# An RWKV block and a gated feed-forward on one core: the constants of the time mixes made on ScalarE, GpSimd started by the norm, and three orders in the attention changed

## The reference, cut to what matters

```python
h  = layer_norm(x, ln1_g, ln1_b)
hh = time_shift(h)                                # the token before
k = (h * tm_mk + hh * (1 - tm_mk)) @ Wk.T         # the three time mixes r, k, v
v = (h * tm_mv + hh * (1 - tm_mv)) @ Wv.T
r = (h * tm_mr + hh * (1 - tm_mr)) @ Wr.T
x = x + sigmoid(r) * wkv(k, v, tm_first) @ Wo.T
h  = layer_norm(x, ln2_g, ln2_b)                  # and two more mixes, cr and ck
kk = (h * cm_mk + hh * (1 - cm_mk)) @ Wkey.T
x = x + sigmoid((h * cm_mr + hh * (1 - cm_mr)) @ Wcr.T) * (silu(kk) @ Wval.T)
x = x + ffn(layernorm(x))                         # silu(gate) * up, then down
```

## Time and profile before

| | us |
|---|---|
| runs | 1052.64, 1053.78, 1054.36 (median 1053.78) |
| profiled execution: own time | 1052.39 |
| its span in the trace | 1050.5 |
| PE busy in the span | 1041.9 |
| DVE, ACT, POOL busy | 704.9, 528.1, 616.7 |

### The profile page before, as it was taken

One profiled execution on the slowest core, in us unless ns is written; L12 is line 12 of the kernel. 1 busy time (PEld: TensorE's weight loads), 2 busy tenths in 40 slices (PEclk: granted clock), 3 DMA queues, 4 the chain that ended last, 5 costly groups with the idle time before them and its releaser, 6 DMA issues.

```text
span 1050.5 us, 13550 instructions
## 1 busy us (share of the span) xinstructions
PE 1041.9 (99%) x4680; PEld 861.8 (82%) x4680; DVE 704.9 (67%) x1215; ACT 528.1 (50%) x889; POOL 616.7 (59%) x508
## 2 busy tenths in 40 slices
PE   8999999999999999999999999999999999999999
PEld 7787888788888888888888888888888888888887
DVE  7899966786545564565459666767698566666655
ACT  7867887866444454323345434343435334444442
POOL 7796574635755545444447755578664356565552
PEclk9999999999999999999999999999999999999999
DMA  9100325177653344742323766575446445444432
GB/s 352 52 21 0 62 80 121 81 230 279 224 190 120 131 160 139 229 150 94 113 88 110 238 218 212 179 234 200 166 156 220 150 151 182 155 156 160 155 107 80
DMA packets 47333, 161.42 MB, mean 154 GB/s; under 512 B 5281, under 2 KB 5665, under 8 KB 42401
## 3 DMA queue, kind: packets, MB, share of 16 engines
q1 hardware_dynamic: 31808, 112.23, 30.8%
q0 software_dynamic: 15168, 48.24, 15.2%
q10 hardware_dynamic: 288, 0.09, 0.0%
HBM read 101.80 MB, written 58.74 MB: 153 GB/s over the span
## 4 chain that ended last, share of the span: by engine, by line
PE 91%; POOL 4%; DVE 3%; ACT 1%; issue 1%; DMA 0%; SPq 0%; DVEq 0%; ACTq 0%
PE bank L634 14%; PE bank L636 14%; PE bank L635 14%; PE bank L623 13%; PE bank L625 13%; PE bank L624 13%; PE bank L812 2%; PE bank L811 2%; PE bank L810 2%; POOL operand L2013 2%; POOL weights L2001 1%; PE bank L801 1%; POOL weights L2013 0%; DVE held L1548 0%; PE bank L698 0%
## 5 line engine op out<-in xcount | busy, mean ns | idle before, releaser
L634 PE MATMUL bank<-combo,left 128*128 128x512 f32 x672 | 262.4, 390 | 0.4 <-DVE bank L1732 0.4
L636 PE MATMUL bank<-combo,left 128*128 128x512 f32 x672 | 261.7, 389 | 0.0
L635 PE MATMUL bank<-combo,left 128*128 128x512 f32 x672 | 261.7, 389 | 0.0
L1663 DVE TENSOR_TENSOR resid<-bank,resid 128x512 f32<-128x512 f32 x176 | 120.6, 689 | 130.2 <-PE bank L625 129.4
L2086 POOL TENSOR_TENSOR inner<-made,inner 128x512 fp32r<-128x512 f32 x96 | 127.7, 1352 | 117.2 <-ACT inner L1135 117.1
L2046 POOL TENSOR_TENSOR left<-quart,left 128x512 fp32r<-128x512 f32 x96 | 115.3, 1225 | 83.6 <-ACT left L1098 43.2
L623 PE MATMUL bank<-right,inner 128*128 128x512 f32 x384 | 149.5, 389 | 0.0
L625 PE MATMUL bank<-right,inner 128*128 128x512 f32 x384 | 149.5, 389 | 0.0
L624 PE MATMUL bank<-right,inner 128*128 128x512 f32 x384 | 149.5, 389 | 0.0
L634 PEld LDWEIGHTS bank<-combo,left 128*128 128x128 f32 x672 | 126.2, 188 | 27.2 <-DVE bank L1732 1.1
L636 PEld LDWEIGHTS bank<-combo,left 128*128 128x128 f32 x672 | 126.2, 188 | 26.2
(11 more groups left out here) (202 smaller groups left out, 1972.8 us busy)
## 6 DMA issues: line engine op xcount, KB each, us to landing
kept_left<-left SPq DMA_DIRECT2D x24, 1792.0 KB, 8.2
left<-kept_left POOLq DMA_DIRECT2D x24, 1024.0 KB, 7.1
left<-kept_left POOLq DMA_DIRECT2D x24, 768.0 KB, 4.9
quart<-wide SPq DMA_DIRECT2D x24, 512.0 KB, 4.2
tall_staged<-tall SPq DMA_DIRECT2D x48, 256.0 KB, 4.9
raw<-kept SPq DMA_DIRECT2D x32, 256.0 KB, 6.2
landed<-wts SPq DMA_DIRECT2D x20, 256.0 KB, 5.5
resid<-x POOLq DMA_DIRECT2D x4, 1024.0 KB, 9.4
```

What stands on the lines that cost most here:

```text
L634: pe.matmul(acc[:], hi, combo[:, c, k, 0, :], start=fresh and k == 0, stop=False, skip_group_check=True)
L635: pe.matmul(acc[:], hi, combo[:, c, k, 1, :], start=False, stop=False, skip_group_check=True)
L636: mm = pe.matmul(acc[:], lo, combo[:, c, k, 0, :], start=False, stop=k == 1, skip_group_check=True)
L1663: dve.tensor_tensor(tile, A[s][:], tile, ALU.add).then_inc(added, 1)
```

## The change

It has five parts.

1. The constants of the mixes r, k and v are made by ScalarE in the new `first_shares`, twelve instructions of 128x3, when the vectors have landed and ahead of `matrix_hi(ITEM_R)`. VectorE makes those of cr and ck and the negated `tm_first` (`vec[:, 4]`) in the new `other_constants`, four instructions, now behind `norm1_moments(1)` and ahead of `mix("v", 0)`; its last line waits until they are done.
2. GpSimd waits for the first norm alone (`z1_ready`) ahead of its low parts of matrix r, and no longer for the constants.
3. In the blocks 2 and 3 ScalarE takes the gates 0 and 1 ahead of `mixed("k", b)`, and 2 and 3 behind it. Block 1 had this order already.
4. Between the third and the fourth `norm1_scaled` of the blocks 2 and 3 VectorE mixes the first tile of r.
5. In the mixes cr and ck of the blocks 0 to 2 VectorE takes the last tokens of the tiles 2 and 3 between the tiles of `mix_ck`, and no longer all ahead of it.

```diff
+FIRST_SHARES = 3 * KT
...
@@ rest_of, on ScalarE
                 act.wait_ge(transposed, KT * b + k + 1)
+                act.wait_ge(const_done, FIRST_SHARES + (4 if kind == "cr" else 0))
...
+            def first_shares():
+                share = vec[:, 5:8, :]
+                for k in range(KT):
+                    act.activation(whole_g[:, 0:3, k], share[:, :, k], ACT.Identity,
+                                   scale=vec[:, 0, k:k + 1]).then_inc(const_done, 1)
+                for k in range(KT):
+                    act.activation(whole_b[:, 0:3, k], share[:, :, k], ACT.Identity,
+                                   scale=vec[:, 1, k:k + 1]).then_inc(const_done, 1)
+                for k in range(KT):
+                    act.wait_ge(const_done, k + 1)
+                    act.activation(rest_g[:, 0:3, k], whole_g[:, 0:3, k], ACT.Identity, bias=vec[:, 0, k:k + 1],
+                                   scale=-1.0).then_inc(const_done, 1)
...
@@ wkv_weight, on ScalarE
                     act.wait_ge(k_psum, n + 1)
+                    act.wait_ge(const_done, FIRST_SHARES + 1)
...
@@ the order on ScalarE
             act.wait_ge(vec_loaded, 16)
+            first_shares()
             matrix_hi(ITEM_R)
-            act.wait_ge(const_done, 3)
+            act.wait_ge(const_done, FIRST_SHARES)
             mixed("r", 0, behind=1, amid=lambda: matrix_hi(ITEM_K, range(1)))
-            act.wait_ge(const_done, 7)
...
                 mix_hi("y", b - 1)
-                if b == 1:
-                    receptance_gate(b, range(2))
-                    mixed("k", b)
-                    receptance_gate(b, range(2, KT))
-                else:
+                if b > 1:
                     act.activation(table[:], minus_half[:, 0, 0:1], ACT.Sigmoid)
-                    mixed("k", b)
-                    receptance_gate(b)
+                receptance_gate(b, range(2))
+                mixed("k", b)
+                receptance_gate(b, range(2, KT))
...
@@ first_norm1, on VectorE
                 for s in range(SUBS):
                     normed(s)
-                shares(slice(0, 3), 0)
+
+            def other_constants():
+                dve.wait_ge(vec_loaded, 16)
                 dve.tensor_scalar(vec[:, 4, :], vec[:, 4, :], NO_STATE, -1.0, ALU.add, ALU.mult).then_inc(const_done, 1)
                 shares(slice(3, 5), 2)
+                dve.wait_ge(const_done, FIRST_SHARES + 4)
...
@@ the order on VectorE
             first_norm1()
             last_of_r_lo()
-            dve.wait_ge(const_done, 7)
+            dve.wait_ge(const_done, FIRST_SHARES)
             mix("r", 0)
...
             norm1_moments(1)
+            other_constants()
             mix("v", 0)
...
-                    norm1_scaled(b + 1, range(2, KT))
-                    mix("r", b + 1)
+                    norm1_scaled(b + 1, range(2, 3))
+                    mix("r", b + 1, range(1))
+                    norm1_scaled(b + 1, range(3, KT))
+                    mix("r", b + 1, range(1, KT))
...
             mix("cr", 0)
-            last_token(1, 0)
-            mix_ck(0)
+            last_token(1, 0, range(2))
+            for k in range(KT):
+                mix_ck(0, range(k, k + 1))
+                last_token(1, 0, range(k + 2, min(k + 3, KT)))
...
@@ the order on GpSimd
             first_norm1()
-            pool.wait_ge(const_done, 7)
+            pool.wait_ge(z1_ready, SUBS)
             matrix_lo(ITEM_R, range(KT - 1))
```

More of the change, by code:

```diff
@@ L1487, in norm1_scaled, with last_token @@
                     dve.tensor_tensor(bank_of, tile, scale, ALU.mult).then_inc(t1_psum, 1)
-            def last_token(norm, b):
+            def last_token(norm, b, tiles=range(KT)):
                 transposed, ms, beta = ((t1_psum, (0, 1, 2), 1), (t2_psum, (3, 4), 3))[norm]
-                for k in range(KT):
+                for k in tiles:
                     dve.wait_ge(transposed, KT * b + k + 1)
@@ L1501, in first_column, with mix @@
                 return (edge[:, b - 1, m, k:k + 1] if b else whole_b[:, m, k:k + 1])
-            def mix(kind, b):
+            def mix(kind, b, tiles=range(KT)):
                 n, m = operand_at(kind, b), MIXES[kind]
@@ L1514, in mix, with mix_ck @@
                                              in1=first_column(b, m, k), op0=ALU.mult, op1=ALU.add).then_inc(op_made, 1)
-            def mix_ck(b):
+            def mix_ck(b, tiles=range(KT)):
                 m = MIXES["ck"]
@@ L1949, in _ @@
             mix("cr", 0)
-            last_token(1, 0)
-            mix_ck(0)
+            last_token(1, 0, range(2))
+            for k in range(KT):
+                mix_ck(0, range(k, k + 1))
+                last_token(1, 0, range(k + 2, min(k + 3, KT)))
             gated_value(BLOCKS - 1)
             mix("cr", 1)
-            last_token(1, 1)
-            mix_ck(1)
+            last_token(1, 1, range(2))
+            for k in range(KT):
+                mix_ck(1, range(k, k + 1))
+                last_token(1, 1, range(k + 2, min(k + 3, KT)))
             mix("cr", 2)
-            last_token(1, 2)
-            mix_ck(2)
+            last_token(1, 2, range(2))
+            for k in range(KT):
+                mix_ck(2, range(k, k + 1))
+                last_token(1, 2, range(k + 2, min(k + 3, KT)))
             for s in range(SUBS):
```

2 lines of the change are left out of this document (1 added, 1 removed).

## The result

The kernel after takes 1055.79 us (median, 1054.60 to 1056.62); runs of before beside it had a median of 1053.77. The ratio is 1.0020, 95% interval 1.0013 to 1.0027: 2.1 us slower (1.4 to 2.8). 1056.7 had been predicted. The profiled execution of after took 1056.51, at the upper end of its runs, that of before 1052.39, near the lower end of its own; the pair differs by 4.12, twice what the medians show. Part of what follows separates the two.

The account below looks back on a forecast made before the run. PE, busy 1041.9 of 1050.5 us, was taken to bound the kernel. The terms 3.2 - 0.46 - 0.50 + 1.1 = +3.3, on the mean of 1053.3, gave 1056.6, stated as 1056.7, range 1053.0 to 1058.6.

Parts of the forecast that it names:

- GpSimd's earlier start: Low parts of matrix r: GpSimd gains 0.6, 0.35 arrives at PE's stop at 26.90, swallowed by the later delay.
- ScalarE's constants: Twelve small activations before the first weight copy take at most 2.4, until 7.2, while ScalarE sat idle: cost 0.
- Constants in front of the mix v: VectorE's four constants delay the mix v by 3.6 beside GpSimd's low parts; PE at 38.58 is 3.2 late.
- three more then wait for one each: After the first constant slips in, three each wait for one GpSimd instruction; the last ends at 31.77 or 0.35 earlier.
- I take back 0.4: Of the mix v's 3.6 delay, 0.4 returns because later VectorE work meets less GpSimd work.
- there is no slack: At 38.58 PE's `g_done` has only just come, so what delays VectorE there delays PE.
- the first rival: The small constants are cheap, costing 0.5 together: +0.3 in all, 1053.6, chance 0.17; decides if the four cost under 2.3.
- Mix between scalings and gates: PE's stops at 94.87 (-0.46, GpSimd's low part earlier) and 104.23 (-0.50, gates ahead of mix k) go.
- Last tokens, block 1: ScalarE's ck parts 2 and 3 wait for tokens, delaying table load, gate and PE at 198.12: +1.1, bounds 0 and 1.3.
- Last tokens, block 2: PE has 96 matmuls, 22 us, before it needs what comes of the ck tiles: 0.
- Block 0: Last tokens there: GpSimd has the whole matrix cr to split before meeting the delay: 0, at most 0.7.
- The sum: All terms together: 3.2 - 0.46 - 0.50 + 1.1 = +3.3 us.

Follow-up runs that it names:

- more constants: The kernel after with the last tokens as before the change, VectorE's three constants of cr and ck made three times over: 1056.69 us, ratio 1.0031.
- tokens back: The kernel after with the last tokens of cr and ck all ahead of mix ck again, as before the change, in all three blocks: 1053.73 us, ratio 1.0001.
- constants and start alone: The kernel before with only the constants moved and GpSimd's earlier start: 1055.24 us, ratio 1.0013.
- tokens in blocks 0 and 2: The kernel before with only the last tokens between the ck tiles, in blocks 0 and 2: 1054.67 us, ratio 1.0012.
- gates and mix: The kernel before with only the two early gates and the mix between the scalings: 1052.40 us, ratio 0.9987.
- constants in front: The kernel after with VectorE's four constants ahead of its low part of matrix r, not in front of mix v: 1056.03 us, ratio 1.0031.

## Why the prediction was right and wrong

The sign was right, and 1055.79 lies in the range; the mechanism of each term was found in the trace, but the largest term was three times too big, and one put at 0 was not 0. That 1056.7 came within 0.9 of the measured time is in part luck: with the constants at their measured 1.1 and the rest as predicted the sum would have been +1.2, and 0.7 of the +2.1 came from a place that the prediction had at 0.

- **GpSimd's earlier start** (0.35 arriving at 26.90, swallowed): right where VectorE's low part goes first, 0.35 and 0.33 by the count above. Not seen was that GpSimd can now start ahead of VectorE's low part and hold it for 0.96. In the profiled execution of after that costs 0.30 at 27.33 and takes the gain back; what is left of its lateness there, 0.43, is about what its data came late (0.45).
- **ScalarE's constants** (0): right. They end at 7.27 and the first weight is copied at 7.85. Each lasts 0.28 to 0.30, as the page "ScalarE: Activation LUTs" of the Trainium skill has it under "Rules for kernel authors"; but they start 0.19 apart, so that twelve take 2.4, the prediction's number, and the 3.6 by that page did not come.
- **Constants in front of the mix v** (+3.2): the failed step is "three more then wait for one each". One waited 1.26 and three passed, so the mix v came 1.5 late (29.40 against 27.91) and not 3.6. The rest of the term held: "I take back 0.4" (1.49 late at the mix v, and 1.10 at the matmul of 38.58), and "there is no slack" (2.82 on VectorE became 2.81 on PE with more constants). The term measures +1.1. The four cost less than the 2.3 below which the first rival was to decide; its own 0.5 was too small too, and 1.5, between its two bounds, is what came. The earlier trace rows were the wrong sample, two rows of instructions in one phase against GpSimd.
- **Mix between scalings and gates** (-0.96): right. -0.57 behind 71 us in the trace of these two alone; -0.87 in the stretch from 71 to 104 us of the run with the tokens back (32.65 against 33.52); -1.4 (0.4 to 2.3) by the times.
- **Last tokens, block 1** (+1.1): right, 1.15 alone and 1.10 in after, with its hole on ScalarE. Most of PE's wait stands at a place that the prediction did not name, ahead of the transposes at 198.61, and ended with the last of the tokens themselves (`edge`, 1.32 idle). The gate behind the table load, the path that it did name, still came last, with 0.27 idle at 201.30.
- **Last tokens, block 2** (0): the failed step is "in block 2 PE has 96 matmuls, 22 us, before it needs what comes of it". That counted the operand of ck only. Queued behind the ck tiles on VectorE are the last block's outputs, which free banks that PE writes 11 us later; that margin was 0.2, and the tokens took 0.9. +0.65 alone, 0.78 in after (3.18 late at 198.12, 3.96 at 209.14). Block 0 (0): right.
- **The sum.** 1.1 - 0.9 + 1.2 + 0.7 = +2.1, which is what was measured. The remaining 2.0 of the 4.12 between the two profiled executions are 1.4 to 1.5 of the long wait at 64 us (PE 1.55 late at 38.58, 1.55 + 1.4 - 0.87 = 2.08 at 104.23), a start that came 0.4 later with its data, and 0.16 that comes between 209 and 262 us, whose cause is open. The prediction took the profile of before, without that wait, as the base of its sum, and then moved it to the mean; that move was right.

What stays open: what decides whether a small instruction passes at a hand-over of GpSimd or not. In the run with the tokens back the offsets started 0.24 behind GpSimd's instruction (63.73 and 63.49) and took 1.10; in that with constants and start alone 0.28 behind (63.89 and 63.61) and took 4.85. At 0.12 behind both occur too: 1.19 in before (62.49 and 62.36) and 4.95 with the tokens in blocks 0 and 2 (62.60 and 62.48). In the run with gates and mix another small instruction waited 4.81 at 56.59, 0.24 behind GpSimd's, there without a stop of PE. No version here beats before by more than the kernel with gates and mix alone.

## What to carry to other kernels

Before moving small SBUF instructions of VectorE, ask what GpSimd does at the new place: beside its elementwise work a 0.16 us instruction takes anything up to GpSimd's whole run, and the number of them counts less than the number of hand-overs they meet. When work is delayed on an engine, follow all that is queued behind it, buffers that it frees for TensorE included, and not only the operand that the moved lines make. And compare traces at fixed matmuls rather than by their spans: one execution with a rare wait can double the difference.

## What the runs showed of the hardware

- A VectorE instruction of 128x8 in SBUF lasts 0.16 alone and 1.20 to 1.26 beside GpSimd's 128x512 subtractions, or passes in 0.15 at a hand-over; two in a row passed at one hand-over (28.33 and 28.39), and one of 128x4 sat out four (4.85, 4.95). The Trainium skill, "SBUF — State Buffer", section "Who interferes with whom", calls the port pair that VectorE and GpSimd share an exclusive lock, and says that the order of issue decides who blocks; the traces agree near 10.4 us, where VectorE's 128x512 took 1.65 when it started behind GpSimd's (after) and 0.69 when 0.07 ahead of it (tokens back). No run here shows why a hand-over is missed.
- In the run with the constants in front TensorE was idle for 1.85 ahead of the first matmul of the attention at 15.04, and its granted clock was 0.66 from 14 to 19 us, partly at 1.2 and partly at 2.4 GHz, and 1.00 again from 19 on. In after it was idle for 0.61 there and the clock stayed at 1.00.
